# A two-layer graph network on one core: the block numbers loaded into VectorE's registers get no range test on the chip

## The reference, cut to what matters

```
h = relu(layernorm(x));  x = x + sage(h)                        # layer 0
h = relu(layernorm(x));  x_l = (h @ W).reshape(N, 4, 32)        # layer 1
logits = leaky_relu(a_src[src] + a_dst[dst] + a_edge, 0.2)      # one per edge and head
m      = segment_max(logits, dst)
p      = exp(logits - m[dst])
out    = segment_sum(p / segment_sum(p, dst)[dst] * x_l[src], dst)
```

## Time and profile before

| What | Value |
|---|---|
| Time, median of 3 runs (lowest to highest) | 3793.0 us (3786.36 to 3794.58) |
| The profiled execution's own time | 3779.88 us |
| Its span, first to last instruction | 3778.0 us |
| Busy share of the span: PE, DVE, ACT, POOL | 86%, 70%, 27%, 51% |
| POOL's first gather of the attention stage begins | 1621.42 us |
| POOL's last gather ends | 3679.36 us |
| Last add of the attention stage ends | 3737.64 us |

### The profile page before, as it was taken

How to read it: one execution, slowest core, us unless ns; L and a number is a source line. 1 busy time by engine, 2 the same in 40 slices (tenths; PEclk the granted TensorE clock), 3 DMA queues, 4 the chain that set the end, 5 groups by cost and what they waited for, 6 DMA issues and landing times. The chain is left out here.

```text
span 3778.0 us, 71084 instructions
## 1 busy us (share of the span) xinstructions
PE 3235.5 (86%) x21900; PEld 2590.8 (69%) x21900; DVE 2631.2 (70%) x7500; ACT 1011.2 (27%) x2337; POOL 1916.0 (51%) x1970
## 2 busy tenths in 40 slices
PE   5799889999998899978888888888888888888884
PEld 5567656777754566557777777777777777777773
DVE  4789999995577544466666666666666666666666
ACT  4455545664200111122222222222222221122220
POOL 5520111521002232167777777777777777777770
PEclk7699999999999999966666666666666666666666
DMA  5233324651366788632222222222222222222254
GB/s 166 93 133 151 127 112 149 165 160 70 104 211 197 205 248 233 182 91 55 55 54 55 54 55 54 55 55 54 55 54 55 55 54 55 54 56 54 55 49 108
DMA packets 148908, 382.00 MB, mean 101 GB/s; under 512 B 39270, under 2 KB 83230, under 8 KB 140450
## 3 DMA queue, kind: packets, MB, share of 16 engines
q0 software_dynamic: 61648, 127.82, 17.5%
q1 hardware_dynamic: 55222, 230.15, 17.0%
q10 hardware_dynamic: 31676, 19.47, 1.7%
HBM read 259.00 MB, written 119.89 MB: 100 GB/s over the span
## 5 line engine op out<-in xcount | busy, mean ns | idle before, releaser
L1917 POOL DMA_INDIRECT G<-x_tab,idx x1620 | 1533.8, 947 | 533.7 <-issue 515.3
L2088 DVE TENSOR_TENSOR ACC<-pu,ACC 128x140 f32 x1650 | 486.8, 295 | 400.5 <-issue 252.9
L2000 PE MATMUL pu<-MSG,OH 128*128 128x140 f32 x3300 | 665.2, 358 | 83.0 <-DVE ACC L2088 78.9
L2000 PEld LDWEIGHTS pu<-MSG,OH 128*128 128x128 f32 x3300 | 576.0, 249 | 109.3 <-DVE ACC L2088 102.8
L1989 PE MATMUL px<-ADG,OHT 128*128 128x4 f32 x3270 | 609.2, 313 | 0.0
L1989 PEld LDWEIGHTS px<-ADG,OHT 128*128 128x128 f32 x3270 | 581.0, 270 | 12.1
L911 PE MATMUL psR<-SPL,AE 128*128 128x384 bf16 x3038 | 566.6, 327 | 0.0
L1610 PE MATMUL psR<-SPL,AE 128*128 128x384 bf16 x3038 | 519.9, 331 | 14.9 <-DMA AE<-a_tab 14.9
L878 ACT CAST AE<-psA 128x784 bf16<-128x784 f32 x496 | 398.3, 813 | 332.3 <-PE psA L901 332.3
L1610 PEld LDWEIGHTS psR<-SPL,AE 128*128 128x128 bf16 x3038 | 299.9, 99 | 213.3 <-DMA AE<-a_tab 17.1
L1937 ACT COPY OHT<-pt 128x512 f32<-128x512 f32 (+1 forms) x436 | 238.6, 558 | 688.2 <-PE pt L1976 686.9
(11 more groups left out here) (410 smaller groups left out, 3150.5 us busy)
## 6 DMA issues: line engine op xcount, KB each, us to landing
a_tab<-AE SPq DMA_DIRECT2D x62, 1568.0 KB, 5.7
AE<-a_tab SPq DMA_DIRECT2D x62, 800.0 KB, 6.4
AE<-a_tab SPq DMA_DIRECT2D x62, 768.0 KB, 5.8
G<-x_tab,idx POOLq DMA_INDIRECT x1620
at_in<-in_edge_attr SPq DMA_DIRECT2D x26, 250.0 KB
room<-in_edge_attr SPq DMA_DIRECT2D x24, 250.0 KB
x_tab<-H ACTq DMA_DIRECT2D x13, 264.0 KB, 4.1
x_keep<-X ACTq DMA_DIRECT2D x13, 256.0 KB, 4.2
```

What stands on the lines that cost most here:

```text
L1917: pool.indirect_dma_start(G[:, u % 3, j, :], None, x_tab, bass.IndirectOffsetOnAxis(ap=idx[:, u % 3, j:j + 1], axis=0)).then_inc(s_g[u % 3 ...
L2000: mm = pe.matmul(pu[:, k[0], k[1]:k[1] + MW], OH[:, u % 4, j, :], MSG[:, u % 2, j, :], start=True, stop=True)
L2088: dve.tensor_tensor(a, pu[:, k[0], k[1]:k[1] + MW][:, None, :], a, ALU.add).then_inc(s_c, 1)
```

## The change

`blocks` gets one more argument, and nothing else in the program changes.

```
     _, v = nc.values_load_multi_w_load_instructions(
-        BLK[0:1, bass.ds(g + 2, 1), at_:at_ + 8], engines=DVE_ONLY, min_val=0, max_val=NB - 1)
+        BLK[0:1, bass.ds(g + 2, 1), at_:at_ + 8], engines=DVE_ONLY, min_val=0, max_val=NB - 1,
+        skip_runtime_bounds_check_because="a block's number counts blocks begun so far, less one")
     blk[at_:at_ + 8] = v
```

## The result

| | before | changed |
|---|---|---|
| Median of the timed runs (lowest to highest) | 3789.68 us (3778.34 to 3794.58, 4 runs) | 3751.34 us (3750.89 to 3758.08, 4 runs) |
| Ratio, 95% interval | | 0.9906 [0.9889, 0.9924] |
| The profiled execution, its span | 3779.88, 3778.0 us | 3758.08, 3756.1 us |
| First gather of the stage | 1621.42 | 1630.93 |
| POOL's last gather ends | 3679.36 | 3669.33 |

The kernel is 0.9% faster; 1.4% was forecast. The profiled execution of the changed kernel was its slowest of four and reached the stage 9.5 us later than the one of before, in stages that the change doesn't touch. So the terms are compared inside the stage, where it took 31.4 us less. The medians lie 38.3 us apart; the 7 us between the two are not traced to anything.

A forecast was written before the change was run, and what follows sets the result against it. DVE and PE together were taken as the bound, POOL a step ahead. Savings of 30 + 18.2 + 1.7 + 4.5 = 54.4 us gave 3725.5 us profiled, 3739 us timed; own range 3731 to 3752, widened to 3727 to 3764.

The forecast's parts named there:

- The tests' cost: DVE's idle time behind the one-hot operation and behind the messages goes: 2.3 and 1.7 us a step.
- The round of DVE and PE: Attention stage without tests: DVE's round about 15.0 us, PE's 16.1 to 16.8, both below POOL's 18.76.
- POOL becomes the bound: Attention loop turns from paced by DVE and PE to paced by POOL, and DVE's lag goes; chance 0.78.
- Term 1: POOL runs all 108 groups without stops at 18.76 us each: 30 us saved, 0 to 32 possible.
- Term 2: DVE's 20.3 us lag behind POOL at the end shrinks to a 2.1 us landing: 18.2 us saved, 11.7 to 19.3.
- a landing of more than 8 us: Sign that the forecast is wrong: gathered data landing over 8 us after POOL is done; 2.1 us was assumed.
- Terms 3 and 4: The stage's end, step 107 and the part behind the loop: 1.7 and 4.5 us saved, 2 to 9 possible.
- term 4: Behind the loop, two calls' tests go, the scaling comes earlier and PE then sets the pace: 4.5 us saved.
- Term 3: Step 107, which no gather follows: 2.15 us idle goes, PE gives back about 0.5; 1.7 us saved.
- the rival of the cold PE: PE loses its warm stretch in each step, its round becomes 21.4 us: slower, about 4040 us; chance 0.05.
- DVE and PE stay the bound: Tests' time turns into waits for PE, POOL still stops, lag stays: 3760 to 3781 us; chance 0.14.
- the tests are hidden anyway: Idle time called issue is really waiting for the gather or PE: within 0.2% of 3793 us; chance 0.03.

The follow-up runs named there:

- e8: Changed kernel with padding edges naming rows 0 to 111 in turn, not all row 0, in a session like the result's: 3736.38 us, ratio to before 0.987.
- e1: The changed kernel run again with nothing altered, in a slow session: 4886.37 us against 4912.25 before, ratio 0.9945.
- e2: Changed kernel with padding edges naming rows 0 to 111 in turn, not all row 0, in a slow session: 4883.89 us, ratio to before 0.9955.

## Why the prediction was right, and where its sizes were off

*The tests' cost.* Right in kind. They were the idle time at both places, 4.0 us a step, and the loads of 1.83 us stay covered. The round shrank by 3.3 us and not by 4.0.

*The round of DVE and PE.* I put it at 16.1 to 16.8 us, since PE was busy for 16.1. It was 15.4 us. The floor I took from PE's busy time was not a floor: at line 1989 the same 3270 matmuls were busy for 473.3 us against 609.2 before. The windows show why, columns as in the earlier trace rows, six microseconds of one step of the kernel before and then of the changed one:

```profile
2507.00:2513.00 6.00, 4.71 (x39) 4.16 (x37) 4.69 (x25) 0.89 (x4) 4.66 (x5) 1.00 0.27 60
```

```profile
2603.00:2609.00 6.00, 5.79 (x49) 5.51 (x49) 5.10 (x27) 2.23 (x11) 4.56 (x5) 1.00 0.24 58
```

By slices of one microsecond the clock stood at its higher level for 6.8 us in either step, and the mean of the stage's body was 0.68 both times. But PE used to wait for DVE inside that stretch and now works through it, 49 matmuls instead of 39, so more of its work ran at the higher clock. The error did no harm, as both values lie under POOL's pace.

*POOL becomes the bound.* Right, shown by the trace of after: no stop from group 3 on, and 348.5 us of DVE waiting for gathers.

*Term 1, POOL without stops: 30 us forecast, 19.5 measured* (2057.9 - 2038.4). Two parts. The group pace over groups 3 to 107 was 18.84 us and not 18.76, which is 8 us. I had read it from six groups of before, in which the gathers' mean was 946 ns (85.12 us in 90); now it was 951 ns. The gathers that ran long (1.0 us instead of 0.94) had become more: 92 over 1 us where 30 had been. And group 2 waited 4.75 us, not 1.97, as the stage's opening took PE longer. PE's timelines, before and then changed, of the same 30 matmuls:

```profile
1649.06 3.73 PE L1989 MATMUL px<-ADG,OHT 128*128 128x4 f32 x30
```

```profile
1658.57 6.40 PE L1989 MATMUL px<-ADG,OHT 128*128 128x4 f32 x30
```

The granted clock over these matmuls was 0.91 before and 0.50 in the changed kernel. That is a matter of which clock level the opening met, not of the change; in e8 they took 3.74 us and the same wait was 1.63 us.

*Term 2, the lag: 18.2 us forecast, 3.8 measured* (20.3 - 16.5). This is the step that was wrong in size, and by far the largest miss. The landing time of 2.1 us that I took was right for groups 5 to 104 (1.7 us in the median) and wrong for the last, the only one that counts. Even my wide end, 8.6 us from the gathers of `OVG`, did not reach 16.5. A stretch read from the middle of a loop was used for its end. e8 shows what the term would have been with ordinary rows: 20.3 - 1.6 = 18.7 us. The prediction had named a landing of more than 8 us as a sign that it was wrong, and for groups 106 and 107 (10.2 and 16.5 us behind POOL) that sign came.

*Terms 3 and 4, the tail: 6.2 us forecast, 8.1 measured* (from the last logits to the last add 37.98 and 29.93 us). From the last messages on it is 15.70 and 11.28 us, so term 4 gave 4.4 where 4.5 were forecast, though not as I had it: PE's last 30 matmuls took 6.27 us, 1.25 for each bank and not 1.5, and the adds came mostly at their own 1.41. Term 3 gave 3.6 and not 1.7. I had counted the call just behind the loop as nothing; DVE's idle time there fell from 3.74 to 1.53 us.

Sum: 19.5 + 3.8 + 8.1 = 31.4 us where 54.4 were forecast. In e8 the stage took 2064.2 us from the first gather to the last add, 52.0 less than before. By terms that is 24.6 + 18.7 + 8.7, so its closeness to the forecast is in part two errors that cancel, a term 1 too large and a tail too small.

*The range.* The ends that the prediction gives its terms (30, 11.7 to 19.3, 2 to 9) add up to 44 to 58 us and not to 41 to 62, so to 3735 to 3749. The measured 3751.3 us lies outside that and inside the range as it was written. With a term 2 of 3.8 us, far below its end of 11.7, that is luck. It helped too that the medians moved by 7 us more than the traced stage.

*The clock.* The rule from "TensorE: Matmul & The Clock Gate" in the Trainium skill, section "HAM oscillation — how this bites in real kernels", would have PE's longer hole end in a slow start. The trace agrees that the step begins at 0.50, but the hole is not what brings the clock down: from 2609.6 on it stood at 0.50 with PE still busy, and the hole opened at 2613.0.

```profile
2609.60:2613.00 3.40, 3.40 (x14) 3.07 (x14) 2.45 (x3) 0.30 (x1) 2.75 (x3) 0.50 0.26 60
```

PE's hole grew to 4.2 us a step, and the granted clock of the stage's body stayed at 0.68. So the rule changed nothing in the time here, and the rival of the cold PE is out.

*The other rivals.* That DVE and PE stay the bound is out: POOL has no stop from group 3 on, and the lag is gone until group 105. That the tests are hidden anyway is out for the result's conditions, since the idle time at both places is gone with them and the time fell by 0.9%. Under the limits of the other sessions it is nearer the truth: there the tests cost 0.1 us a group (28.78 against 28.67) and some 12 us at the stage's end, since the stall took up the rest.

## What to carry to other kernels

When a cheap edit frees one engine, read how far the others can follow: here 3.3 us a step were set free, and POOL's unbroken chain of gathers let only 0.2 us of it through, plus the end. A wait that nobody feels can be long in coming to light: look at the DMA share to the end of a stage, for what is late behind a later engine turns into the bound once that engine is on time. And pad a gather's index list with different rows, not with one row's number throughout.

## What the runs showed of the hardware that I had not expected

- An indirect gather of 128 rows of 528 bytes kept the DMA engines busy for four times as long when all 128 numbers were the same: share 0.96 against 0.24, 41 GB/s against 55; within one session 0.75 against 0.17 (e1 and e2). Thirty-two of them in a row fell 14.8 us behind POOL's 1.25 us each, so they took about 1.7 us apiece.
- In three of four sessions DVE's first add of a group waited until 2.3 to 2.7 us after the end of POOL's gathers, and some signals from PE to ACT came late as well. ACT's timeline of e1, a copy that by the code waits for PE's transposes of lines 1976 and 1979 (done at 3001.94) and for DVE's masks (done at 2990.6):

```profile
3011.22 0.26 ACT L1936 COPY KT<-pt 60x128 f32<-60x128 f32 x1 [7.12 <-issue]
```

  In the stretch in which POOL issued nothing (3012.14 to 3022.01) DVE had no such stall. Not every signal was late while it issued: a copy of ACT followed PE's transposes at 2999.03 at once. The same program was 30% slower in these sessions. The fourth session, on one of the same chips, had none of it. What differed between the sessions is open; no run tells it.
- A test of one loaded number cost DVE's sequencer two instructions, 183 + 23 ns by the records and about 0.3 us by the starts. Eight numbers came to 2.1 to 2.5 us in the two calls of one step, more than the load of all eight (1.83 us).
